# A top-32 attention block: the mask in a 16-bit buffer, the softmax sum folded into ScalarE's exponent, and all engine orders written out as strings

## What is computed

```python
scores = jnp.einsum('bthd,bghd->bhtg', Q, K) / np.sqrt(DH).astype(np.float32)
scores = jnp.where(vision_mask[:, None, None, :], scores, -jnp.inf)
topv, topi = jax.lax.top_k(scores, K_TOP)
probs = jax.nn.softmax(topv, axis=-1)
attn = jnp.zeros_like(scores).at[bi, hi, ti, topi].set(probs)
attn_mean = attn.mean(axis=1)
c_t = jnp.einsum('btg,bgd->btd', attn_mean, V)
```

## Time and profile before

| | us |
|---|---|
| median of 3 executions | 1715.34 |
| lowest, highest | 1712.01, 1718.7 |
| span of the profiled execution | 1709.8 |

### The profile page before, as it was taken

How to read it: one execution, slowest core, us unless ns; L and a number is a source line. 1 busy time by engine, 2 the same in 40 slices (tenths; PEclk the granted TensorE clock), 3 DMA queues, 4 the chain that set the end, 5 groups by cost and what they waited for, 6 DMA issues and landing times.

```text
span 1709.8 us, 22306 instructions
## 1 busy us (share of the span) xinstructions
PE 1512.3 (88%) x7299; PEld 1119.8 (65%) x7307; DVE 1382.8 (81%) x2241; ACT 1135.8 (66%) x2069; POOL 1152.1 (67%) x1267
## 2 busy tenths in 40 slices
PE   5887878798978897889999999999999899999996
PEld 3454655565656564667776777776776667667896
DVE  7798979997999899988898898889898999344321
ACT  3589955786578667866887678866886578322442
POOL 1498956757875887689768986798579858501322
PEclk8897989897989998999999999999999999999998
DMA  7200130002100210123313231322232112483431
GB/s 220 69 4 4 24 102 19 25 19 62 31 25 20 62 31 25 31 68 97 97 49 91 72 87 49 102 72 62 71 96 63 50 56 59 141 278 96 94 51 22
DMA packets 97223, 115.26 MB, mean 67 GB/s; under 512 B 17840, under 2 KB 74168, under 8 KB 96964
## 3 DMA queue, kind: packets, MB, share of 16 engines
q1 hardware_dynamic: 85348, 100.32, 20.2%
q0 software_dynamic: 11760, 13.52, 5.2%
HBM read 75.48 MB, written 19.58 MB: 56 GB/s over the span
## 4 chain that ended last, share of the span: by engine, by line
PE 36%; DVE 26%; ACT 16%; POOL 13%; issue 7%; DMA 1%; SPq 1%; POOLq 0%; DVEq 0%
DVE R L1500 8%; DVE ZB L1504 6%; PE PS L2371 4%; POOL ZB L779 3%; PE PS L2224 3%; DVE ZB L1496 3%; ACT ZB L1076 3%; PE PS L2248 3%; PE PS L1946 3%; DVE R L1456 2%; ACT R L1082 2%; PE PS L2176 2%; PE PS L1996 2%; PE PS L2177 2%; DVE R L1492 2%
## 5 line engine op out<-in xcount | busy, mean ns | idle before, releaser
L1500 DVE MAX8 R<-ZB 128x8 f32<-128x1024 f32 x384 | 471.0, 1227 | 10.3
L1504 DVE MATCH_REPLACE8 ZB<-R,ZB 128x1024 f32<-128x1024 f32 x256 | 309.5, 1209 | 0.0
L1946 PE MATMUL PS<-R 128*128 128x256 f32 x1048 | 277.9, 396 | 14.1 <-ACT R L1079 10.7
L779 POOL TENSOR_TENSOR ZB<-ZB 128x1024 f32<-128x1024 f32 x95 | 230.0, 2421 | 85.7 <-ACT ZB L1076 85.5
L1079 ACT ACTIVATE R<-PS 128x512 f32<-128x512 f32 (+6 forms) x404 | 172.4, 464 | 130.6 <-PE PS L2186 30.3
L1946 PEld LDWEIGHTS PS<-R 128*128 128x128 f32 x1048 | 198.6, 198 | 60.7 <-issue 17.0
L781 POOL TENSOR_TENSOR ZB<-ZB 128x1024 f32<-128x1024 f32 x95 | 224.2, 2360 | 7.5
L1492 DVE MAX8 R<-PS 128x8 f32<-128x1024 f32 x128 | 156.0, 1219 | 27.0 <-PE PS L1969 26.9
L1076 ACT ACTIVATE R<-R 128x32 f32<-128x32 f32 (+2 forms) x356 | 96.9, 273 | 96.8 <-DVE R L1500 28.2
L1496 DVE MATCH_REPLACE8 ZB<-R,PS 128x1024 f32<-128x1024 f32 x128 | 155.5, 1215 | 0.0
L1076 ACT ACTIVATE ZB<-ZB,R 128x1024 f32<-128x1024 f32 x128 | 147.1, 1149 | 4.2
(11 more groups left out here) (284 smaller groups left out, 3123.6 us busy)
## 6 DMA issues: line engine op xcount, KB each, us to landing
ZR<-ZR SPq DMA_DIRECT2D x96, 128.0 KB
ZB<-in_L_ffn_rt_gate SPq DMA_DIRECT2D x21, 512.0 KB, 4.2
ZB<-in_L_ffn_rt_up SPq DMA_DIRECT2D x21, 512.0 KB, 5.3
ZB<-in_L_ffn_rt_down SPq DMA_DIRECT2D x21, 512.0 KB, 4.6
R<-in_x SPq DMA_DIRECT2D x16, 512.0 KB, 4.2
ZB<-in_ctx SPq DMA_DIRECT2D x8, 768.0 KB, 4.9
R<-xs_d SPq DMA_DIRECT2D x39, 128.5 KB, 2.1
out<-R SPq DMA_DIRECT2D x32, 128.0 KB, 2.7
```

Source lines behind the costliest of these rows:

```text
L779: pool.tensor_tensor(e, e, w, ALU.mult).then_inc(s.g_att, 1)
L1500: vec.max(ml[:, 8 * r:8 * r + 8], w).then_inc(s_tk[n % 2], 1)
L1504: vec.match_replace(w, ml[:, 8 * r:8 * r + 8], w, NEG).then_inc(s_tk[n % 2], 1)
L1946: pe.matmul(q_bank(*key)[:, 0:256], ident, warm, start=True, stop=True)
```

## The change

On ACT the step list of a tile becomes seven steps in two generators, `attention` (five) and `masks` (two). The exponent of all scores now comes after the search, with the sum inside it: exp(SCALE * score - SCALE * max - ln(sum)). The mask is 1 or 0 in one 16-bit buffer `keep` for all tiles, so Relu of tile n waits until POOL has multiplied tile n - 1. PE's scores wait for both readers of tile n - 2. DVE's search no longer waits for POOL, and `limits` is gone. The due times and tables are gone: each engine has a string with one character per step, and PE one digit per step for fillers. Besides, `actx` now lies in `att`.

```diff
+        keep = alloc_b(512).bitcast(BF16)
...
 # POOL
-        pool.tensor_tensor(e, e, w, ALU.mult).then_inc(s.g_att, 1)
+        pool.tensor_tensor(e, e, keep, ALU.mult).then_inc(s.g_att, 1)
...
 # ACT
+            def masks():
+                for n in range(16 * B):
+                    yield
+                    on.wait_ge(s_tk[n % 2], PASS * (n // 2) + 7)
+                    on.wait_ge(s.g_att, taken(n - 1))
+                    act.activation(keep, sc_bank(n), ACT.Relu, bias=mx[n % 3][:, 31:32], scale=-1.0).then_inc(s.a_keep, 1)
+                    yield
+                    on.wait_ge(s.a_keep, 2 * n + 1)
+                    exp(keep, keep, ACT.Exp, scale=-STEEP).then_inc(s.a_keep, 1)
...
-                    yield tile_at(n) + ACT_EXP[n % 16]
-                    on.wait_ge(s_tk[n % 2], PASS * (n // 2) + 2)
-                    on.wait_ge(s.v_limit, 2 * n + 1)
-                    on.wait_ge(s.g_att, added(n - 2))
-                    exp(e, sc_bank(n), ACT.Exp, bias=q[:, 0:1], scale=SCALE).then_inc(s.a_att, 1)
-                    yield tile_at(n) + ACT_SUM[n % 16]
+                    yield
+                    on.wait_ge(s_tk[n % 2], PASS * (n // 2) + 1)
+                    on.wait_ge(s.a_att, 5 * (n - 3) + 5)
+                    copy(q[:, 0:1], ml[:, 0:1], scale=-SCALE).then_inc(s.a_att, 1)
+                    yield
                     on.wait_ge(s_tk[n % 2], PASS * (n // 2) + 7)
+                    on.wait_ge(s.a_att, 5 * n + 1)
                     exp(junk, ml, ACT.Exp, bias=q[:, 0:1], scale=SCALE, accum_out=q[:, 1:2]).then_inc(s.a_att, 1)
-                    yield tile_at(n) + ACT_GAP[n % 16]
-                    act.activation(w, sc_bank(n), ACT.Relu, bias=ml[:, 31:32], scale=-1.0).then_inc(s.a_att, 1)
-                    yield tile_at(n) + ACT_CUT[n % 16]
-                    on.wait_ge(s.v_limit, 2 * n + 2)
-                    exp(q[:, 3:4], q[:, 2:3], ACT.Ln).then_inc(s.a_att, 1)
+                    yield
+                    on.wait_ge(s.a_att, 5 * n + 2)
+                    exp(q[:, 2:3], q[:, 1:2], ACT.Ln).then_inc(s.a_att, 1)
+                    yield
+                    on.wait_ge(s.a_att, 5 * n + 3)
+                    affine(q[:, 3:4], q[:, 2:3], scale=-1.0, bias=q[:, 0:1]).then_inc(s.a_att, 1)
+                    yield
                     on.wait_ge(s.a_att, 5 * n + 4)
-                    exp(w, w, ACT.Exp, bias=q[:, 3:4], scale=-STEEP).then_inc(s.a_att, 1)
+                    on.wait_ge(s.g_att, added(n - 2))
+                    exp(ee[n % 2], sc_bank(n), ACT.Exp, bias=q[:, 3:4], scale=SCALE).then_inc(s.a_att, 1)
...
 # DVE
-                    on.wait_ge(s.g_att, taken(n - 2))
                     vec.match_replace(w, ml[:, 0:8], sc_bank(n), NEG).then_inc(s_tk[n % 2], 1)
...
-            def limits():
-                for n in range(16 * B):
...
-                    TS(q[:, 0:1], ml[:, 0:1], -SCALE, None, ALU.mult).then_inc(s.v_limit, 1)
...
-                    vec.reciprocal(q[:, 2:3], q[:, 1:2]).then_inc(s.v_limit, 1)
...
 # PE
-                    on.wait_ge(s.a_att, 5 * (n - 2) + 3)
+                    on.wait_ge(s.a_att, 5 * (n - 2) + 5)
+                    on.wait_ge(s.a_keep, 2 * (n - 2) + 1)
```

More of the change, by code:

```diff
@@ new lines, in ring_keys @@
+def ring_keys():
+    return dict(
+        finish=[("finish", t, k) for t in range(4 * B) for k in range(4)],
+        prep=[("prep", b, use) for b in range(B) for use in range(NP)],
+        weights=[("weight", 0, k) for k in range(6)],
+        kernel_values=[("chunk", ch, k) for ch in range(8) for k in range(2)],
+        post=[("post", b, use) for b in range(B) for use in range(RANK) if b < B - 1 or use not in range(FILM_OUT, FILM_OUT + 4)],
+        film_out=[("post", B - 1, FILM_OUT + i) for i in range(4)],
+        ranks=[("post", b, use) for b in range(B) for use in (RANK, COUNT) if use == RANK or b in dict(PASSES)],
+        shared=[("post", b, use) for b in range(B) for use in range(SHARED, NQ)],
+        tiles=[("tile", j, use) for j in range(FULL) for use in (T_TURN, T_GATE, T_UP, T_DOWN)])
@@ L294, with __init__, weave @@
+lay_ring()
+class Clock:
+    def __init__(self):
+        self.step = -1
+def weave(order, clock, *parts):
+    for p in parts:
+        next(p)
+    for c in order:
+        clock.step += 1
+        next(parts[int(c, 36)], None)
 class Waits:
@@ L390, in flamingo_kernel @@
         mx = [alloc(32) for _ in range(3)]
-        sm = [alloc(5) for _ in range(3)]
+        sm = [alloc(4) for _ in range(3)]
         small = [alloc(116) for _ in range(2)]
@@ L736, in _ @@
             setup()
-            weave(inputs(), contexts(), queries(), keys(), kernel_rows(), late(), post(), tiles(), routed())
+            weave(SP_ORDER, Clock(), inputs(), contexts(), queries(), keys(), kernel_rows(), late(), post(), tiles(), routed())
         @block.gpsimd
@@ L1938, in _, with keep_warm @@
             on = Waits(pe)
-            def keep_warm(count, key):
+            clock = Clock()
+            def keep_warm():
+                count, key = int(PE_WARM[clock.step]), NEXT_BANK[clock.step]
                 if count:
```

723 lines of the change are left out of this document (319 added, 404 removed), and 10 rows, old and new, of tables (DVE_TOP, POST_AT).

## The result

The changed kernel takes 1669.03 us (median of 4 executions, 1663.21 to 1671.78) against 1716.91 us (4 executions, 1712.01 to 1718.70): a ratio of 0.972, with a 95% interval of 0.970 to 0.974. It is 48 us faster; the forecast was 1676 us.

A forecast was written before the change was run, and what follows sets the result against it. DVE was taken to bound the kernel, with the other engines near. Removed waits 8 + 27 us and small operations 4 made 39: 1709.8 - 39 = 1671 profiled, plus 5.5 for the median, 1676 us; own range 1650 to 1703, 8-in-10 range 1634 to 1713.

The forecast's parts named there:

- Removed waits: DVE's waits for ACT's sum and POOL's read of the search buffer, 56.2 us, go; 35 us of them kept.
- The two shares: Kept parts of DVE's removed waits: a half of 15.6 us before 761 us, two thirds of 40.6 behind it.
- Where it comes: Late batches save most, 27 us, through PE's room from fewer fillers; before 761 us only 8 us.
- Small operations: 256 one-column instructions leave DVE: 4 of some 5 us saved; the skill's whole-time reading gives 37.6 us.
- Fillers: On PE, 240 of 524 go; 20 us could leave the chain, not counted, but PE lets a faster DVE through.
- The banks: Score banks come free 2.2 us later per tile, behind ACT's logarithm, sum and exponent; costs 1 us a batch.
- the rival at 1738: Slower: the later release of the banks passes through PE whole, 10.5 us a batch, 84 in all; 10%.
- The one mask buffer: ACT's Relu waits for POOL's product of the tile before; costs nothing, or 30.6 us if POOL's room is gone.
- POOL's product: With one 16-bit operand it still takes 2421 ns; the ends are -10 to +4 us of POOL's 140 per batch.
- Clock: PE's granted clock stays at 0.94 or more from 761 us; rival: fewer fillers lower it, no gain, 1712, 6%.
- Head and tail: The tail keeps its work and most of its order; nothing counted, last search to end within 4 us of 255.
- That the order was rewritten: PE's order, 292 of 889 steps out of the common sequence, can move each stage by a few microseconds either way.

The follow-up runs named there:

- old late fillers: The changed kernel with the filler counts of the kernel before from score tile 64 on, 461 instead of 279: 1719.5 us.
- early exponent: The changed kernel with the exponent of all scores ahead of the sum instead of behind it, the division by the sum left out: 1674.3 us.
- path alone: The changed data path in the orders of the kernel before, with its 524 fillers: 1796.9 us, ratio 1.047 to the kernel before.

## Why the prediction was right, and where it wasn't

The total came in 7 us under the forecast: a saving of 42.9 us between the profiled executions against 39 in the sum. That it came so near is in good part luck: 12 of the 42.9 us lie in head and tail, where the sum had nothing, the late batches gave 9 us where it had most of its 39, and the early ones 22 where it had 8.

**Removed waits** (the sum: 27 of 40.6 us kept after 761 us, 8 of 15.6 before). Over the whole program about half was kept, 27 of 56 us, by DVE's waits, where the sum kept 35. That waits come back as waits for PE, "DVE gets to its next tile sooner, and PE, ACT and POOL will now and then not be there", is what happened. What fails is that the sum takes the share from the engines' loads and leaves the order out: in the old orders nothing was kept, and with late exponent and single mask both undone the path stands at 1726.0 us, with 56.7 us of new waits for PE. The two shares, named as what no row gives, came near in size for the whole change and had no mechanism behind them.

**Where it comes** (27 us in batches 4 to 7, "13 to 15 us less per late batch", 8 before). It was 9 us in the late batches (2.4, 5.1, 1.0 and 0.6) and 22 in the early ones. That PE would not let a faster DVE through before 761 us is refuted. The room in the late batches was read too large: fillers of 20.1 us went from batch 5, PE's busy time fell by 12.7 us, and its granted clock from 0.99 to 0.96. The 137 us of needed work were the total less the fillers, which leaves out that their records overlap with others. Why DVE did not use even the 12.7 us, no run shows.

**Small operations** (4 of 5 us, 37.6 by the other reading). With them back the time is 1665.3 against 1669.0 us. The reading of the gaps was right in kind; for operations that wait for nothing the term should have been nothing. (The two of the kernel before did wait, for ACT and for the first pass, and that part is among the removed waits.)

**Fillers** (not in the sum; "the reason why PE lets a faster DVE through"). Confirmed as a condition for these orders: with the old late fillers the whole gain is gone, 50 us and not the 20 that their share of the chain suggested. Not confirmed as a cause that stands alone: the same cut costs 15 to 16 us in the old orders.

**The banks** (1 us a batch; the rival at 1738). In the orders that came with the change it holds: the early exponent gains nothing. PE's wait for the last readers went from 17.9 to 33.4 us, DVE's for scores from 26.9 to 39.8, inside the 25 to 45 forecast. The banks came free 2.9 us later behind the sum in the mean (4.2 against 1.3), not 2.2. In the old orders the rival is real, with 16 to 30 us for the exponent. What the runs show to decide is not DVE's lead, as I wrote, but which order the path runs in.

**The one mask buffer** (nothing; 30.6 if its cover were gone). ACT's Relu waits 22.2 us for POOL, where "under 10 us" was to be seen, so the cover is thinner than I took it. In the old orders it costs 40.5 to 54.8 us, more than the upper end.

**POOL's product** ("2.3 to 2.5 us", ends at -25% and +10%). 2176 ns, 10% less: under that range and within the ends of the sum. It is the 16-bit operand, since with a 32-bit mask in the new orders the product takes 2426 ns. The 16-bit output costs ACT nothing, as the row had it (Relu 1105 ns, before 1104), and the dropped bias gives 96 ns per mask exponent, in 16 bits (1053 ns) as in 32 (1054). ACT's new one-column operations were counted at 200 ns each and take 197 and 292.

**Clock.** 0.94 or more from 761 us on: batches 4 to 7 have 0.94, 0.96, 0.94 and 0.99, down from 0.99 to 1.00. It held, with nothing to spare, and the run without fillers shows lower clocks (0.877 over the program) and a longer time.

**Head and tail** ("I count nothing there"; tail within 4 us of 255). The head is 5.9 us shorter. From the last search pass to the end it took 255.6 us before and takes 249.9, 5.7 less and outside the 4. Stages that have no search in them got shorter as well; that is 12 of the 42.9 us and the largest term left out. The path alone doesn't do it (head 69.0, tail 257.9), and with the old late fillers the tail takes 258.8, so its gain needs the new orders and their counts.

**That the order was rewritten** stood in the forecast as "a few microseconds either way". It was the term that mattered most. From the path alone (1796.9) to the change (1669.0) orders and fillers together are worth 128 us; the orders with the old late fillers (461 in all, the early ones those of the change) are worth 77. The change is no sum of a data path and an order. The path alone loses 81 us; with the new orders and counts it gains 48.

**Still open.** Which moves of the new orders carry the 77 us, and how the old data path would do in them: that part of the gain, or all of it, would come to the old path too is a rival that no run excludes. Against it stands only that one part undone, the mask's buffer, costs 124 us there. That DVE begins a tile early at 37 places instead of 16, of which 30 (8 before) lie in the first four batches, where most of the gain came, fits, but no run tests it. What makes 182 fillers harmful at the new places and useful at the old ones was not followed either, beyond the waits that they bring back.

## What to carry over

A change of data path and the order it runs in are one change: price the new release times in the old order first, where they may cost more than the removed waits bring. Here the order, with its filler counts, decided the sign. Before counting a removed wait as saved time, ask which engine is next to be late at the same place; here it was PE, with 29 us of new waits for 56 removed in the new orders and 57 in the old ones. The best number of fillers belonged to an order: the same cut cost 16 us in one and gained 50 in the other.

## What the hardware showed that was not expected

- A one-column operation of DVE that waits for nothing starts while the 1.22 us pass ahead of it is still running (454.50 against an end of 454.58), and two of them fit into the gap in front of the next dependent pass: 1.258 us with and 1.257 without over 82 places.
- POOL's product of 128x1024 takes 2421 ns with two 32-bit operands and 2176 ns when one has 16 bits, its output having 32 bits in both; with the mask in 32 bits again it takes 2426 ns.
- An ACT operation of one column takes 197 ns without a bias read from memory and 292 ns with one; the mask exponent over 1024 columns takes 1149 ns with and 1053 ns without. The Trainium skill (ScalarE: Activation LUTs, What ACT_TABLE_LOAD costs) gives about 93 ns for such an operand, and the trace agrees with 95 and 96 ns.
- 177 fewer fillers in the kernel before, where PE was busy for 88% of the span, lowered the granted clock of the profiled execution from 0.955 to 0.940 and made the median 16 us slower; in batches 5 to 7 it fell from 0.99 or 1.00 to 0.93 or 0.94.
